# Gated attention block with a top-8 router: two buffers for the turned blocks, router rows turned by TensorE, new slots

## The reference

```
h   = layernorm(x, over the 2048 positions)
per window of 128 positions:
    q = Wq h + bq;  k = Wk h + bk;  v = Wv ctx + bv          # 256 channels, 8 heads of 32
    a = softmax(q^T k / sqrt(32), masked)                     # 128 x 128 for each head
    o = gelu(a v);  out = (Wo o + bo) * mask                  # 512 channels
x1  = x + tanh(g_xattn) * out
f   = layernorm(x1, over the 2048 positions)                  # one token for each of the 512 channels
s   = softmax(f Wr^T + rb)                                    # 64 experts
w   = the 8 largest of s, the others zero
y   = x1 + tanh(g_ffn) * (f * sum(w) + w @ expert_bias)
```

## Time and profile before

| | |
|---|---|
| median of three runs | 1323.04 us (1320.90 to 1323.36) |
| the profiled execution: time, span of the trace | 1328.39 us, 1326.4 us |
| TensorE (PE) busy | 1123.9 us, 85% |
| ScalarE (ACT) busy | 1004.8 us, 76% |
| VectorE (DVE) busy | 968.2 us, 73% |
| GpSimd (POOL) busy | 871.4 us, 66% |
| transfers PT<-T | 992 of 112 KB and 32 of 80 KB |
| DMA bytes | 232.27 MB, mean 175 GB/s |
| granted TensorE clock, mean | 0.963 of full speed |

### The profile page before, as it was taken

The page is one execution under the profiler, slowest core; times in us unless marked ns, Lnnn a source line. Parts: engine busy times, 40 slices in busy tenths (PEclk is TensorE's granted clock), DMA queues, the critical chain, the costliest instruction groups (busy, mean ns, idle before and its releaser), DMA issues.

```text
span 1326.4 us, 32364 instructions
## 1 busy us (share of the span) xinstructions
PE 1123.9 (85%) x11165; PEld 1010.7 (76%) x11165; DVE 968.2 (73%) x1859; ACT 1004.8 (76%) x3072; POOL 871.4 (66%) x784
## 2 busy tenths in 40 slices
PE   3779899888898888897888899898989879889857
PEld 3668788878887777787877788787878778878745
DVE  6647768877589766888578876788658876688546
ACT  4767788877789588787879778887778858888743
POOL 2457778567785577856776678756777557775631
PEclk9899999999999899999999999989999989999979
DMA  9395555796557955588656966579555795557543
GB/s 275 105 209 143 137 139 144 182 291 154 143 138 215 259 131 144 141 268 214 147 140 145 290 182 149 135 194 281 144 144 137 229 250 132 143 135 220 138 109 127
DMA packets 169763, 232.27 MB, mean 175 GB/s; under 512 B 27776, under 2 KB 104704, under 8 KB 169472
## 3 DMA queue, kind: packets, MB, share of 16 engines
q1 hardware_dynamic: 168736, 230.19, 66.3%
q10 hardware_dynamic: 864, 0.01, 0.0%
HBM read 80.06 MB, written 33.65 MB: 86 GB/s over the span
## 4 chain that ended last, share of the span: by engine, by line
SPq 36%; DVE 18%; PE 12%; DMA 10%; ACT 10%; issue 9%; POOL 5%; DVEq 0%; ACTq 0%; POOLq 0%
SPq L551 33%; DMA PT<-T 8%; ACT P L643 7%; DVE T L797 5%; DVE T L806 2%; POOL ht_lo L1118 2%; DVE X L936 2%; DVE o L812 2%; DVE nmx L790 2%; DMA cx<-in_ctx 1%; ACT L643 1%; PE ring L475 1%; SPq L556 1%; PE ring L343 1%; DVE bnst L946 1%
## 5 line engine op out<-in xcount | busy, mean ns | idle before, releaser
L643 ACT ACTIVATE P<-ring,nmx 128x128 f32<-128x128 f32 x1024 | 360.6, 389 | 2.1 <-DVE nmx L790 1.3
L328 PE MATMUL ring<-z_hi,wqk_hi 128*128 128x256 f32 x1024 | 302.1, 295 | 24.8 <-DVE z_lo L1000 21.1
L329 PE MATMUL ring<-z_hi,wqk_lo 128*128 128x256 f32 x1024 | 294.3, 287 | 0.0
L330 PE MATMUL ring<-z_lo,wqk_hi 128*128 128x256 f32 x1024 | 294.1, 287 | 0.0
L797 DVE STREAM_TRANSPOSE T<-P 128x512 f32<-128x512 f32 x256 | 170.8, 687 | 135.9 <-DMA PT<-T 134.9
L1106 POOL TENSOR_TENSOR X<-X,xt 128x512 f32<-128x512 f32 x128 | 165.2, 1291 | 153.1 <-DVE xt L825 152.1
L1118 POOL TENSOR_TENSOR ht_lo<-PT,ht_hi 128x512 fp32r<-128x512 f32 x124 | 160.1, 1292 | 133.7 <-ACT ht_hi L667 133.5
L643 ACT ACTIVATION_READ_ACCUMULATOR P<-ring,nmx 128x1 f32 x1024 | 234.5, 229 | 0.0
L328 PEld LDWEIGHTS ring<-z_hi,wqk_hi 128*128 128x128 f32 x1024 | 200.9, 196 | 38.9 <-DVE wqk_lo L975 21.1
L643 ACT ACT_TABLE_LOAD x62 | 79.5, 1283 | 171.0 <-DVE nmx L790 171.0
L825 DVE SCALAR_TENSOR_TENSOR xt<-ring,cst,mg 128x256 f32<-128x256 f32 x256 | 111.5, 477 | 131.3 <-PE ring L405 131.0
(11 more groups left out here) (139 smaller groups left out, 2806.9 us busy)
## 6 DMA issues: line engine op xcount, KB each, us to landing
PT<-T SPq DMA_DIRECT2D x992, 112.0 KB, 2.3
cx<-in_ctx SPq DMA_DIRECT2D x128, 256.0 KB, 3.8
out_y<-X SPq DMA_DIRECT2D x128, 256.0 KB, 4.4
X<-in_x SPq DMA_DIRECT2D x112, 256.0 KB, 4.9
mg<-in_mask SPq DMA_DIRECT2D x64, 128.0 KB, 3.8
X<-in_x SPq DMA_DIRECT2D x8, 512.0 KB, 7.5
sel<-rows_d SPq DMA_DIRECT2D x256, 3.0 KB
PT<-T SPq DMA_DIRECT2D x32, 80.0 KB, 2.6
```

The source lines that it names most:

```text
L328: e.matmul(o, wqk_hi[:, t, cols], z_hi[:, t, :], t == 0, False)
L329: e.matmul(o, wqk_lo[:, t, cols], z_hi[:, t, :], False, False)
L330: last = e.matmul(o, wqk_hi[:, t, cols], z_lo[:, t, :], False, t == DT - 1)
L643: last = e.activation(P[:, n, :], bank("S", 4 * u + g)[:, k * W:(k + 1) * W], ACT.Exp, bias=nmx[u % 2][:, n:n + 1], accum_out=den[u % 2][: ...
```

## The change

- T becomes two buffers, T[0] and T[1], chosen by the unit's parity. `turn_p(u)` and `turn_d(u)` now wait for the landing of unit u-2, not u-1. P and PT stay single.
- T and PT shrink from 28 to 20 blocks. The transfers are 16 a unit as before, of 80 KB.
- `turn_h` goes. For all 64 units TensorE turns X with 8 transposes of 128x128 (`r_turn`), into two PSUM banks out of the ring of seven. ScalarE makes ht_hi from the bank, VectorE makes ht_lo from it (before: POOL).
- `o32` has two buffers, not three. `move` no longer waits for `htlo_g` and `turn`.
- All numbers in SLOTS and ENDS are new. `after` with its 14.75 late slots goes: logits, top-8, mix, stores and loads of a batch stand about one unit earlier.

```
-        T = sb("T", [128, 4, 28, 32])
-        PT = sb("PT", [128, 4, 28, 32])
+        T = [sb(f"T{i}", [128, 4, 20, 32]) for i in range(2)]
+        PT = sb("PT", [128, 4, 20, 32])
 ...
             def move(u):
                 e.wait_ge(td_v, u + 1)
                 if u:
                     e.wait_ge(on_v, u)
-                if u > HLAG:
-                    e.wait_ge(htlo_g, 2 * (u - HLAG))
-                n = 28 if u >= HLAG else 20
-                if u >= HLAG:
-                    e.wait_ge(turn_v, u - HLAG + 1)
                 for b in range(4):
                     for a in range(4):
-                        e.dma_start(PT[32 * b:32 * b + 32, a, 0:n, :], T[32 * a:32 * a + 32, b, 0:n, :]).then_inc(pt_in, 16)
+                        e.dma_start(PT[32 * b:32 * b + 32, a, :, :], T[u % 2][32 * a:32 * a + 32, b, :, :]).then_inc(pt_in, 16)
 ...
             def turn_p(u, g):
-                if u:
-                    e.wait_ge(pt_in, 256 * u)
+                if u >= 2:
+                    e.wait_ge(pt_in, 256 * (u - 1))
 ...
             def r_high(u, a):
-                if u < TF0:
-                    e.wait_ge(pt_in, 256 * (u + HLAG + 1))
-                    e.activation(by_block(ht_hi[a][:]), turned(a), ACT.Copy).then_inc(hthi_a, 1)
-                else:
-                    e.wait_ge(ht_pe, n - 2 * TF0 + 1)
-                    e.activation(by_block(ht_hi[a][:]), blocks(bank("hT", n)[:]), ACT.Copy).then_inc(hthi_a, 1)
+                e.wait_ge(ht_pe, n + 1)
+                e.activation(ht_hi[a][:], bank("hT", n)[:], ACT.Copy).then_inc(hthi_a, 1)
 ...
             def r_low(u, a):                                   # VectorE
                 e.wait_ge(hthi_a, n + 1)
+                e.tensor_tensor(ht_lo[a][:], bank("hT", n)[:], f32(ht_hi[a][:]), ALU.subtract).then_inc(htlo_v, 1)
 ...
-                for u in due(t, C["turn"], count=TF0):
-                    turn_h(u)
 ...
-            def r_low(u, a):                                   # POOL
-                e.tensor_tensor(by_block(ht_lo[a][:]), turned(a), by_block(f32(ht_hi[a][:])), ALU.subtract).then_inc(htlo_g, 1)
 ...
-    norm2=29.75, c_base=37.25, L=33.75, LT=34, c_top=39.5, ... mix=43, m_gap=0.75,
+    norm2=29, c_base=37.5, L=36.25, LT=33, c_top=38.75, ... mix=43.25, m_gap=0.25,
```

More of the change, by code:

```diff
@@ L42 @@
 SLOTS = dict(
[L44 to L59, removed]
+    rows=-28.5, z32=-26.5, z_hi=-15.5, z_lo=-19.75, q=-15.5, q_ev=-7.5, k=-9.5, k_ev=-6.25,
+    c_hi=-14.75, c_lo=-14.75, v=-12.5, v_ev=-7, v_gap=-2.25,
+    S=-2.25, top=1.5, exp=4, e_gap=0.25, tp=6.25, td=8.25, mv=9.25, PV=21.5, on=24.25,
+    gelu=24.25, mg=4.25, ot_hi=24.25, ot_lo=24.25, WO=26.75, WO_gap=4.25, xt=29.75, x1=31, bn2=41.25,
+    hT=35.5, hT_gap=0.5, ht_hi=39.75, ht_lo=42, R=47,
+    norm2=29, c_base=37.5, L=36.25, LT=33, c_top=38.75, c_exp=39.25, c_w=41, c_sc=42.5, wT=40.25, wt_hi=44, wt_lo=44.5, mix=43.25, m_gap=0.25,
+    sx=47.75, sx_gap=0.25, x2=45.75, rl=51.5, rl_gap=0.75,
+    x_1=26.5, x_gap=3, bn1=60.5, bn1_gap=2, norm1=97.5,
 )
 ENDS = {
[5 rows of a table removed]
[5 rows of a table added]
 }
@@ L290, in gated_block_kernel @@
                 for u in units(t, "hT", C["hT_gap"] * a):
-                    if u >= TF0:
-                        take(("hT", 2 * u + a), t, end("ht_lo", u) - end("hT", u), htlo_v, 2 * (u - TF0) + a + 1)
-            for b in after(t, C["LT"]):
+                    take(("hT", 2 * u + a), t, end("ht_lo", u) - end("hT", u), htlo_v, 2 * u + a + 1)
+            for b in batch(t, C["LT"]):
                 take(("LT", b), t, C["c_top"] - C["LT"], lg_v, b + 1)
-            for b in after(t, C["wT"]):
+            for b in batch(t, C["wT"]):
                 take(("wT", b), t, C["wt_lo"] - C["wT"], wtlo_v, b + 1)
             for i in range(16):
-                for b in after(t, C["mix"] + C["m_gap"] * i):
+                for b in batch(t, C["mix"] + C["m_gap"] * i):
                     take(("mix", b * 16 + i), t, C["x2"] - C["mix"], x2_v, b * 16 + i + 1)
@@ L593, in _ @@
                 for i in range(16):
-                    for b in after(t, C["x2"] + C["m_gap"] * i):
+                    for b in batch(t, C["x2"] + C["m_gap"] * i):
                         store(b, i // 4, i % 4)
-                    for b in after(t, C["rl"] + C["rl_gap"] * i):
+                    for b in batch(t, C["rl"] + C["rl_gap"] * i):
                         if b + 2 < NB:
@@ L803, in turn_d @@
                 e.wait_ge(rden_v, u + 1)
[L804 to L806 removed]
+                if u >= 2:
+                    e.wait_ge(pt_in, 256 * (u - 1))
+                e.transpose(T[u % 2][:, :, 16:20, :], rden[:].rearrange("p (b k) -> p b k", b=4).unsqueeze(3).to_broadcast([128, 4, 4, 32])).then_inc(td_v, 1)
             def divide(u):
@@ L1066, in _ @@
                     w_low(b)
-                for b in after(t, C["c_sc"]):
+                for b in batch(t, C["c_sc"]):
                     if b < NB - 1:
@@ L1157, in _ @@
                         add_x(u, j)
-                for a in range(2):
-                    for u in due(t, C["t_lo"] + C["t_gap"] * a, count=TF0):
-                        r_low(u, a)
                 for b in batch(t, C["norm2"]):
```

80 lines of the change are left out of this document (22 added, 58 removed), and 10 rows, old and new, of the table ENDS.

## The result

| kernel | median, us | lowest to highest | runs |
|---|---|---|---|
| before | 1323.2 | 1320.9 to 1323.88 | 4 |
| after | 1253.44 | 1251.46 to 1255.94 | 4 |

The ratio is 0.9477 with a 95% interval of 0.9451 to 0.9502: 70 us faster. The profiled execution took 1251.46 us, its span is 1249.7 us. I had predicted 1277 with a range of 1245 to 1325, from a saving of 46 us.

A forecast was written before the change was run, and what follows sets the result against it. It took the transfer loop over single T, 17.3 us a unit, as the bound. From the profiled 1328.4 us, 40 for quiet units and 6 for turns gave 1282; the median, 5.3 lower, 1277 us, range 1245 to 1325.

The forecast's parts named there:

- Rival D: A larger gain: quiet units reach the loop over the exponentials, 16.4 us, 1248 us in total; chance 0.10.
- loop (a): Loop over the exponentials: GELU, WO, scores, maxima, 16 exponentials, reciprocals, division, back to GELU; 16.35 us a unit.
- A: Rival, slower: the new transposes stall TensorE, a unit takes 18.8 us, 1365 us in total; chance 0.12.
- B: Rival, no gain: the batch's turn gives all 46 us back, 1323 us; chance 0.08.
- C: Rival, smaller gain: transposes don't overlap, a unit takes about 17.6 us, 1308 us in total; chance 0.10.
- the quiet unit, 17.1: Forecast length of a unit outside the turns, down from 18.06 us; 40 us saved over 42 units.
- the 0.75: Excess of the old quiet unit, 18.06 us, over its 17.3 us loop of transfers, added to the exponentials' 16.35.
- (b): TensorE's work in one unit: 14.7 us of matmuls plus the eight new transposes, 15.8 us.
- The batch's turn, -6 us: Long units at each batch change: -2 for smaller transfers, +1.1 for transposes and stores, over 7 turns.
- Their number costs, not their size: SP's 16 transfers a unit: 10.55 us to issue at 112 KB, 11.40 at 80 KB, so narrowing gains nothing in quiet units.
- Units run at this loop: Over single T: issue 9.96, landing 2.23, VectorE's turns to reciprocals 5.10, in sum 17.3 us a unit, nothing overlapping.
- The covers: TensorE's 5.3 us of other work hides the transposes' 4.9 us wait for POOL's addition to X, by 0.4 us.

The follow-up runs named there:

- less_pe: Changed kernel with 6 of the 24 matmuls that make k left out; 1251.93 us, ratio 0.9476 to the kernel before.
- one_T_wide: Changed kernel with a single T, and T, PT and the transfers as wide as before (112 KB); 1306.7 us, ratio 0.9879 to the kernel before.
- one_T: Changed kernel with a single T again, all else as changed; 1279.95 us, ratio 0.9692 to the kernel before.
- norm2_early: Changed kernel with the second norm's small operations moved 3.5 slots forward (29 to 25.5); 1250.68 us, ratio 0.944 to the kernel before.

## Why the prediction was right, and where its steps failed

**The sign and the size.** 1253.4 lies in the range and 24 us under the forecast. Rival D (quiet units at loop (a), 1248) is what happened in quiet units, and I had given it 0.10. A, B and C didn't happen: eight transposes took 1.04 us in the record and 0.87 in the list, no matmul waits 1 us in each unit for a bank or for X, and the turn gave nothing back.

**Where the missing 29 us lie.** Between the first and the last reciprocal I had forecast 46 us and 75.5 were measured. In 35 quiet units and seven turns of four units, the forecast comes to 35 x 0.96 = 34 and 7 x 0.96 + 6 = 13; measured are 57 and 18. So 23.6 of the missing 29 us lie in the quiet units and 5.6 in the turns. My own split has 42 units and seven turns of three. If the last three long units are taken as the turn, the 42 went from 757.7 to 721.2 us, 36.5 less where I said 40, and the turns from 469.9 to 431.0, 39 less where I said 6. The hit on 40 is luck: seven of the 42, the first of each turn, became 2.95 us longer, since more of the router's work now lies there. I had not foreseen a fourth long unit.

**The term that was mis-sized: the quiet unit, 17.1.** It measured 16.26 in 25 units and 16.42 in the mean of 35. The loop (a), 16.35, was right to 0.1 us, and the 0.75 that I added for friction was the error: 35 x (17.1 - 16.42) = 24 us. I had read it off the old loop over T and carried it to another loop. (a) has the right length with a wrong link: I went from the exponentials over the reciprocals and o to GELU; less_pe's chain goes over ScalarE's two copies and its table load. (b), 15.8, measured 15.92. That TensorE might idle for 2.0 us was wrong; that idle time belonged to the loop over T and went with it.

**The batch's turn, -6 us.** I had three parts: +1.1 for the transposes and the stores, -1.8 for the smaller transfers, from 0.5 MB at 292 GB/s, and nothing for the second buffer. The steps from before over one_T_wide and one_T to the changed kernel are +3.6, -2.9 and -3.4 us a turn. Each is larger than I had it, and since they have both signs the errors cancel in part. The size counts at the turn because the wide transfers land there in 6.15 to 8.48 us beside loads and stores of X; the second buffer counts because the transfers start late behind loads of X, which one T hands on to the next unit. "Their number costs, not their size" is true of the issue and was read off a quiet unit.

**The mechanism.** "Units run at this loop" fits the kernel before, but the whole gain was credited to the second buffer. one_T has a single T and nearly the same row of waits (130.6 us), and gets 1.35 of the 1.64 us a quiet unit. The prediction counted X's turn, 1.21 us, among the parts of the loop and then did not take it out when it asked what one buffer would do.

**The covers.** The transposes wait for X five times, 4.7 us in all; in the quiet unit shown X is ready at 634.40 and they start at 636.31, so the cover was 1.9 us there and not 0.4. The start moved by 1.2 us and the tail by 0.1, and the unit with the additions stayed at 25.3 to 26.7.

## What to carry to other kernels

List the parts of a loop one by one and strike out each that the change removes, before a second buffer is credited with its slack; the sum of the waits does not price it, as the row stayed at 130.6 us in a kernel 40 us faster. Check a small wait against the time at which the thing waited for was done: 26.9 us stood here under transfers that had landed long before. Where two loops lie 0.3 us apart, the chain names only the last engine: add work to one and take work from the other, and read the lengths of the units. An in-order queue that carries both urgent transfers and transfers with a wait makes the urgent ones late; look for what stands ahead of the urgent ones, at the turns most of all.

## What the runs showed of the hardware

Three of VectorE's small operations over 128x4 values take many times their length when they start beside a large one on GpSimd. Two of them at a turn of the changed kernel, what GpSimd did beside the first, and the second again in the tail of the same execution:

```profile
644.58 2.18 DVE L808 TENSOR_SCALAR ln<-mv 128x4 f32<-128x4 f32 x1
...
651.02 1.13 DVE L827 TENSOR_TENSOR gate<-gate,ln 128x4 f32<-128x4 f32 x1
```

```profile
644.37 2.36 POOL L1045 TENSOR_TENSOR z_lo<-z,z_hi 128x1024 fp32r<-128x1024 f32 x1 [1.54 <-ACT z_hi L581]
```

```profile
1227.43 0.16 DVE L827 TENSOR_TENSOR gate<-gate,ln 128x4 f32<-128x4 f32 x1
```

2.18 us, and it ends (646.75) when GpSimd's subtraction does (646.73). norm2_early moves this operation away from the subtraction, and there it takes 0.17 us in all eight batches:

```profile
644.98 0.17 DVE L808 TENSOR_SCALAR ln<-mv 128x4 f32<-128x4 f32 x1
```

L827 takes 1.12 to 1.13 us in seven turns, beside POOL's addition to X, and 0.16 in the tail. L847 takes 1.09 or 1.10 us in the three turns in which it starts beside POOL's cx_lo, and 0.17 in the five batches in which it doesn't. In the Trainium skill, the "GPSIMD Engine Reference" (Key points) says that the two engines share their interfaces to SBUF and contend in a two-port mode of VectorE or where it has two inputs from SBUF; the rows agree that they contend, and show that the small operation waits for the whole of the large one. Which of the two conditions L808 meets, no run here shows.

A group of 8 transposes on TensorE is recorded with 1.04 us and one of 16 with 1.91, so a further 128x128 transpose costs 0.109 us where it follows another, though the single one is recorded with 279 ns.
